# Weight matrices laid out partition by partition in DRAM, in a two-stage transformer kernel on eight cores

## The reference

```
mod = silu(c) @ wmod                       # six vectors per sequence: sa, ca, ga, sb, cb, gb
h = layernorm(x) * (1 + ca) + sa
x = x + ga * ttt(h)       # K, V, Q = h @ thetas; scan with W, b updated per token
h = layernorm(x) * (1 + cb) + sb
x = x + gb * ffn(h)
  ttt step:  g = 2/1024 * (W k + b - v);  W -= 0.01 * outer(g, k);  b -= 0.01 * g;  out = W q + b
  ffn:       routed = top-2 of 8 experts, y = (silu(h @ gate) * (h @ up)) @ down, weighted by the softmax scores
             shared = the same with matrices of inner width 2048
```

## Time and profile before

| | us |
|---|---|
| median of three runs | 1615.85 |
| the three runs | 1603.39, 1615.85, 1644.12 |
| the profiled execution | 1616.92 |
| its span, slowest core (core 3) | 1615.3 |
| cores 1, 5, 7 (second role) | 1612.0, 1609.5, 1596.2 |
| cores 0, 2, 4, 6 (first role) | 1535.8, 1546.6, 1536.4, 1550.9 |

### The profile page before, as it was taken

One profiled execution on the slowest core, in us unless ns is written; L12 is line 12 of the kernel. 1 busy time (PEld: TensorE's weight loads), 2 busy tenths in 40 slices (PEclk: granted clock), 3 DMA queues, 4 the chain that ended last, 5 costly groups with the idle time before them and its releaser, 6 DMA issues.

```text
span 1615.3 us, 22747 instructions; the slowest of 8 cores (1535.8 to 1615.3 us)
## 1 busy us (share of the span) xinstructions
PE 1417.2 (88%) x7825; PEld 703.9 (44%) x7825; DVE 738.8 (46%) x1278; ACT 493.8 (31%) x784; POOL 304.0 (19%) x209
## 2 busy tenths in 40 slices
PE   0587899798968998999997899999797999989897
PEld 0343444344444444444543444644343444434354
DVE  2426555647444456457447423432122222222576
ACT  1144444345444444444434321122121111101010
POOL 0058875803300001001011110000000000000131
PEclk9999999899989999999998999999899999999999
DMA  9954356616457522122172659397999999974763
GB/s 238 265 114 136 105 151 125 156 53 169 85 131 137 157 66 92 53 92 76 43 170 92 169 126 239 105 221 146 213 194 210 170 202 224 180 157 173 272 209 131
DMA packets 82373, 244.16 MB, mean 151 GB/s; under 512 B 7365, under 2 KB 7493, under 8 KB 77638
## 3 DMA queue, kind: packets, MB, share of 16 engines
q0 software_dynamic: 47440, 112.75, 35.2%
q1 hardware_dynamic: 26870, 92.05, 17.2%
q10 hardware_dynamic: 7936, 37.75, 9.5%
HBM read 262.46 MB, written 78.64 MB: 211 GB/s over the span
## 4 chain that ended last, share of the span: by engine, by line
PE 71%; DMA 13%; DVE 8%; issue 5%; POOL 1%; ACT 1%; another core or an unknown queue 1%; SPq 0%; DVEq 0%; POOLq 0%; ACTq 0%
PE prep L664 9%; PE u L928 7%; PE gate L897 5%; PE u L826 5%; PE up L897 5%; PE up L894 5%; PE gate L894 5%; PE prep L928 4%; PE up L729 3%; PE up L756 3%; DMA w1u<-uw 3%; PE gate L729 3%; DMA w1u<-suw 3%; PE gate L746 2%; DMA wmb<-wmod 2%
## 5 line engine op out<-in xcount | busy, mean ns | idle before, releaser
L1416 DVE TENSOR_TENSOR act<-up,sgb 128x512 bf16<-128x512 f32 (+1 forms) x128 | 84.0, 658 | 317.1 <-PE up L897 194.6
L1084 ACT ACTIVATE sgb<-gate 128x512 bf16<-128x512 f32 (+1 forms) x128 | 73.0, 570 | 466.1 <-PE gate L897 228.2
L1292 DVE TENSOR_TENSOR WT<-WT,u 128x512 f32<-128x512 f32 x240 | 153.4, 679 | 52.3 <-PE u L826 52.0
L826 PE MATMUL u<-Gsb,Ktk 128*128 128x512 bf16 x480 | 129.7, 394 | 41.9 <-DVE WT L1292 40.8
L664 PE MATMUL prep<-hft,s_thK 128*128 128x512 bf16 x512 | 124.3, 391 | 7.5 <-ACT hft L993 3.4
L1054 ACT CAST Wbf<-WT 128x1024 bf16<-128x1024 f32 x120 | 124.7, 1041 | 14.7 <-DVE WT L1292 14.6
L1603 POOL DMA_INDIRECT hx<-h2m,sl x28 | 29.1, 1038 | 447.4 <-DVE sl L1399 441.8
L826 PEld LDWEIGHTS u<-Gsb,Ktk 128*128 128x128 bf16 x480 | 44.0, 100 | 99.5 <-issue 63.9
L1545 POOL TENSOR_SCALAR x2b<-x2b,silc 128x1024 f32<-128x1024 f32 x28 | 80.1, 2862 | 23.6 <-DMA x2b<-wmod 22.5
L664 PEld LDWEIGHTS prep<-hft,s_thK 128*128 128x128 bf16 x512 | 50.5, 100 | 72.2 <-issue 18.9
L746 PE MATMUL gate<-Wbf,Kft 128*128 128x512 bf16 x256 | 80.8, 391 | 0.0
(11 more groups left out here) (250 smaller groups left out, 2318.2 us busy)
## 6 DMA issues: line engine op xcount, KB each, us to landing
hx<-zero ACTq DMA_DIRECT2D x4, 5120.0 KB, 30.6
x2b<-wmod POOLq DMA_DIRECT2D x32, 512.0 KB, 5.1
yx<-ring SPq DMA_DIRECT2D x32, 512.0 KB, 5.9
xb<-x SPq DMA_DIRECT2D x22, 512.0 KB
wmb<-wmod SPq DMA_DIRECT2D x8, 1024.0 KB, 12.1
x2b<-x SPq DMA_DIRECT2D x16, 512.0 KB, 4.6
hx<-zero ACTq DMA_DIRECT2D x4, 2048.0 KB, 11.4
pair<-gw POOLq DMA_DIRECT2D x4, 2048.0 KB, 29.2
```

Of the source, the lines that this page charges most:

```text
L826: m = t.matmul(U[jh][:, 0:512], Ktk[s % 2][:, cc * D + dt * P:cc * D + (dt + 1) * P], Gsb[:, cc * D + jh * 512:cc * D + (jh + 1) * 512], s ...
L1292: v.tensor_add(w, w, U[jh][:, 0:512]).then_inc(S["v_W"], 1)
L1416: v.tensor_mul(act[k % 2][:, fj * ACW:fj * ACW + COLS[k]], R[2 + n % 2][:, 0:COLS[k]], sgb[n % 2][:, 0:COLS[k]]).then_inc(v_act, 1)
```

## The change

The weight matrices are rearranged on the host: for each matrix `[1024, 1024]`, row `128 * dt + p` moves to row p, column `1024 * dt` of a matrix `[128, 8192]`. The shared matrices are first cut in halves. Each load then reads one contiguous run of 32 KB for each partition, and W0, loaded in two parts, runs of 16 KB. What arrives in SBUF, its place, the DMAs, their order and their waits stay as they are.

```diff
-    d_thK = nc.dram_tensor("thK", [D, D], F32, kind="ExternalInput")
+    d_thK = nc.dram_tensor("thK", [P, DT * D], F32, kind="ExternalInput")
...
-    d_gw = nc.dram_tensor("gw", [NE, D, D], F32, kind="ExternalInput")
-    d_sgw = nc.dram_tensor("sgw", [D, 2 * D], F32, kind="ExternalInput")
+    d_gw = nc.dram_tensor("gw", [NE, P, DT * D], F32, kind="ExternalInput")
+    d_sgw = nc.dram_tensor("sgw", [2, P, DT * D], F32, kind="ExternalInput")
...
                 for i in range(2):
                     g.dma_start(WT[:, 4 * i * D:4 * (i + 1) * D],
-                                ap(d_w0T, 4 * i * P * D, [[D, P], [P * D, 4], [1, D]])).then_inc(ld_w0, 16)
+                                ap(d_w0T, 4 * i * D, [[DT * D, P], [1, 4 * D]])).then_inc(ld_w0, 16)
...
                 def w_matrix(u, dst, which, done):
                     if u in (0, NE + 1):
-                        half = 0 if u == 0 else 1
-                        t, row, first = ((d_sgw, 2 * D, half * D), (d_suw, 2 * D, half * D),
-                                         (d_sdw, D, half * D * D))[which]
+                        t, i = (d_sgw, d_suw, d_sdw)[which], (0 if u == 0 else 1)
                     else:
-                        t, row, first = (d_gw, d_uw, d_dw)[which], D, (u - 1) * D * D
-                    g.dma_start(ap(dst, 0, [[DT * D, P], [D, DT], [1, D]]),
-                                ap(t, first, [[row, P], [P * row, DT], [1, D]])).then_inc(done, 16)
+                        t, i = (d_gw, d_uw, d_dw)[which], u - 1
+                    g.dma_start(ap(dst, 0, [[DT * D, P], [1, DT * D]]),
+                                ap(t, i * D * D, [[DT * D, P], [1, DT * D]])).then_inc(done, 16)
...
         def w_cast(g, dst, src, done):
-            g.dma_start(ap(dst, 0, [[DT * D, P], [D, DT], [1, D]]),
-                        ap(src, 0, [[D, P], [P * D, DT], [1, D]])).then_inc(done, 16)
+            g.dma_start(ap(dst, 0, [[DT * D, P], [1, DT * D]]),
+                        ap(src, 0, [[DT * D, P], [1, DT * D]])).then_inc(done, 16)
...
+    def by_partition(a):
+        a = np.asarray(a, dtype=np.float32)
+        t = a.reshape(a.shape[:-2] + (DT, P, D))
+        return np.ascontiguousarray(np.moveaxis(t, -3, -2)).reshape(a.shape[:-2] + (P, DT * D))
+    def halves(a, axis):
+        return np.stack(np.split(np.asarray(a, dtype=np.float32), 2, axis=axis))
```

More of the change, by code:

```diff
@@ L280, in build_program @@
     d_wmod = nc.dram_tensor("wmod", [D, 6 * D], F32, kind="ExternalInput")
-    d_thK = nc.dram_tensor("thK", [D, D], F32, kind="ExternalInput")
-    d_thV = nc.dram_tensor("thV", [D, D], F32, kind="ExternalInput")
-    d_thQ = nc.dram_tensor("thQ", [D, D], F32, kind="ExternalInput")
-    d_w0T = nc.dram_tensor("w0T", [D, D], F32, kind="ExternalInput")
+    d_thK = nc.dram_tensor("thK", [P, DT * D], F32, kind="ExternalInput")
+    d_thV = nc.dram_tensor("thV", [P, DT * D], F32, kind="ExternalInput")
+    d_thQ = nc.dram_tensor("thQ", [P, DT * D], F32, kind="ExternalInput")
+    d_w0T = nc.dram_tensor("w0T", [P, DT * D], F32, kind="ExternalInput")
     d_b0 = nc.dram_tensor("b0r", [1, D], F32, kind="ExternalInput")
     d_rw = nc.dram_tensor("rw", [D, NE], F32, kind="ExternalInput")
-    d_gw = nc.dram_tensor("gw", [NE, D, D], F32, kind="ExternalInput")
-    d_uw = nc.dram_tensor("uw", [NE, D, D], F32, kind="ExternalInput")
-    d_dw = nc.dram_tensor("dw", [NE, D, D], F32, kind="ExternalInput")
-    d_sgw = nc.dram_tensor("sgw", [D, 2 * D], F32, kind="ExternalInput")
-    d_suw = nc.dram_tensor("suw", [D, 2 * D], F32, kind="ExternalInput")
-    d_sdw = nc.dram_tensor("sdw", [2 * D, D], F32, kind="ExternalInput")
+    d_gw = nc.dram_tensor("gw", [NE, P, DT * D], F32, kind="ExternalInput")
+    d_uw = nc.dram_tensor("uw", [NE, P, DT * D], F32, kind="ExternalInput")
+    d_dw = nc.dram_tensor("dw", [NE, P, DT * D], F32, kind="ExternalInput")
+    d_sgw = nc.dram_tensor("sgw", [2, P, DT * D], F32, kind="ExternalInput")
+    d_suw = nc.dram_tensor("suw", [2, P, DT * D], F32, kind="ExternalInput")
+    d_sdw = nc.dram_tensor("sdw", [2, P, DT * D], F32, kind="ExternalInput")
     d_zero = nc.dram_tensor("zero", [P, D], BF16, kind="ExternalInput")
@@ L1897, in make_inputs @@
     f32 = lambda a: np.ascontiguousarray(np.asarray(a, dtype=np.float32))
+    def by_partition(a):
[4 more added lines that the diff above has]
+        return np.stack(np.split(np.asarray(a, dtype=np.float32), 2, axis=axis))
     base = {
[L1899 to L1902, removed]
+        "thK": by_partition(np.asarray(L0_attn_theta_K).T),
+        "thV": by_partition(np.asarray(L0_attn_theta_V).T),
+        "thQ": by_partition(np.asarray(L0_attn_theta_Q).T),
+        "w0T": by_partition(np.asarray(L0_attn_W0).T),
         "b0r": f32(np.asarray(L0_attn_b0).reshape(1, D)),
         "rw": f32(L0_ffn_router_w),
-        "gw": f32(L0_ffn_gate_w), "uw": f32(L0_ffn_up_w), "dw": f32(L0_ffn_down_w),
-        "sgw": f32(L0_ffn_shared_gate_w), "suw": f32(L0_ffn_shared_up_w),
-        "sdw": f32(L0_ffn_shared_down_w),
+        "gw": by_partition(L0_ffn_gate_w), "uw": by_partition(L0_ffn_up_w), "dw": by_partition(L0_ffn_down_w),
+        "sgw": by_partition(halves(L0_ffn_shared_gate_w, 1)), "suw": by_partition(halves(L0_ffn_shared_up_w, 1)),
+        "sdw": by_partition(halves(L0_ffn_shared_down_w, 0)),
         "wmod": f32(L0_wmod),
```

## The result

| | before | after |
|---|---|---|
| median, 20 runs each | 1614.49 us | 1627.60 us |
| ratio of the changed kernel to the kernel before | | 1.0075, 95% interval 1.0051 to 1.0100 |
| span of core 3, the slowest, in the profiled execution | 1615.3 us | 1625.0 us |

Within 2%, but clearly on the other side of no change than was forecast. The ratio is that of undisturbed executions; in others one die or both run at a lower granted clock and end some per cent later.

A forecast was written before the change was run, and what follows sets the result against it. The prediction took the second role's cores, with TensorE waiting for late expert weights, to bound the kernel. It summed -12.6 - 2.3 + 2 - 3 = -15.9, from 1616.9 to 1601 us, range 1578 to 1628 (8 in 10).

The forecast's parts named there:

- What bounds the kernel: Second role's cores end last; in the expert stage TensorE waits 18.4 us and 4.8 us for late w1u loads.
- (a) Cost per packet: Weight loads on POOL's queue: memory, not packets, sets the pace, so fewer packets save 0.
- (b) Share of turns: Late weight bursts beside SP and ACT: weights hold 86% of turns, waits shrink 12.6 us, slow matmuls behind them 2.3.
- (c) What waits longer, ring: x2 rows read back to the ring: a row tile stands behind weight turns, +2 us (0 to +8).
- (c) token rows: Experts' token-row loads behind weight turns: 42 us, then the rest runs free, within 46.3 us of cover; it fits.
- the prediction's own signs of being wrong: Lone burst's bytes per us move over 5%, TensorE waits at hxb's transposes, or VectorE's ring wait grows over 8 us.
- (d) The start: VectorE's modulation sums at the start: thK lands sooner, second wmod tile about 5 us sooner; -3 us, bounds -5 and +3.5.
- nothing changes: Rival for the whole kernel: runs cut again into some 4 KB packets, or memory's pace hides all; 1616 us, chance 0.28.
- slower memory order: Rival in weight bursts: reads from places 32 KB apart cost a sixth of the pace; +40, 1657 us, chance 0.09.
- Full relief: Rival in late bursts: long sequential reads win back the other 5 us, all waits go; -35.2, 1582 us, chance 0.17.
- Starved token rows: Rival in the experts: unpausing weight turns make token loads 57 us, +10 us in each of seven; 1672 us, chance 0.05.
- VectorE's wait for ring grows by more than 8 us: A sign that would show the prediction wrong, at VectorE's wait for x2 rows read back, 5.6 us once before.

The follow-up runs named there:

- e6: Changed kernel, but only thK, thV, thQ and W0 keep long runs; expert and shared matrices in separated 4 KB rows; ratio to the kernel before 0.9975.
- e3: Changed kernel's layout with a 256 B gap behind each 4 KB row, so no read is longer; ratio to the kernel before 0.9997.
- e4: Changed kernel with units 1 and 2 (first two experts) in separated 4 KB rows, other matrices in 32 KB runs; 1599.4 us, 0.9899 of the kernel before.
- e9: Changed kernel with e1's three waits on POOL's queue and each partition's token rows made one piece; ratio to the kernel before 0.9921.
- e1: Changed kernel with three more waits on POOL's queue, issuing weights of units 1 and 2 later, apart from x2 tiles; 1607.6 us, 0.9970 of the kernel before.

## Why the prediction was wrong, point by point

- **What bounds the kernel**: right. The late bursts were TensorE's only DMA waits of size in the expert part, and they went: 23.2 to 3.7 us.
- **(a) Cost per packet, taken as 0**: right, as far as it shows: 4.5 to 5.7 MB in 30 us of a burst before, 4.6 to 5.7 after.
- **(b) Share of turns, -12.6 and -2.3**: the mechanism was right, the turns are one for one, and beside SP and ACT the queue moved 4.92 MB in 36 us against 4.75 in 30 nearly alone, 86%, the forecast share. It measured -19.5 us of waits and, in the experts' stretch, -13.2 with the wait of 3.2 us for hxb in it. The forecast took 4.2 us from each late burst; measured, all but 3.7 us of the 23.2 went, so the weights' share of the turns was worth about half as much again. Why it is more than the turns account for I did not separate; that a burst no longer begins late behind another late one is argued only. That a wait as short as 0.6 us spares the slow matmuls held: behind the wait of 0.3 us for `w0u` eight took 1.89 us, the usual time in this timeline. Behind 3.41 us they took 3.54.
- **(c) What waits longer, ring, +2 (0 to +8)**: here it failed. The wait for ring grew by 28.0 us and the stage by 28.6. The sum priced one tile, eight packets per engine, against weights that it took for passing by. At the first place SP has five tiles queued, 40 packets per engine, beside 24 long turns, and one of its tiles lands only at 950.27 + 44.57 = 994.8 us. The sum counted 24 turns for the token rows and only eight here; with 24 x 1.77 = 42 us it would have had this wait. At the second, the finished tile in a place of the ring must be written out before the next is read into it, both through SP's queue beside the next burst: 28.9 us from issue to landing, a wait of 20.3. The row that it rested on, 5.6 us, was read as a bound on the effect, though it only showed how little was to spare.
- **(c) token rows, no cost**: nearly. 24 x 1.77 = 42 us was the forecast for a landing behind a whole burst; 42.6 was measured once, with 3.2 us of wait. But the cover of 46.3 us was that of a step with a wait of 9.7 us and its slow matmuls in it. In a plain step it is 34.2: issue at 1194.53, first transpose at 1228.74 in the kernel before. At the place of the new wait it was 39.6, since the wait for `w1u` fell into it, and the load took 42.6. That TensorE waits there was one of the prediction's own signs of being wrong.
- **(d) The start, -3**: wrong in sign, small in size. thK did land sooner (20.0 us for 29.5), but by the code SP's queue has five loads of eight packets per engine (the first x rows and four of constants) ahead of the first wmod tile, and they too take turns with thK: the x rows let VectorE start some 3.5 us later, the tile came at 27.7 and not at 21.5. The wait before the second tile fell to 2.8, as forecast, only because the first came late. No run separated this. The sums end at 61.0 us in place of 58.4, 2.6 later, and the difference is lost in the scatter of the scan (947.2 against 949.3). e6 shows no loss.
- **The rivals**: *nothing changes* failed at the packet count; *slower memory order* failed at e3 and at the pace of the bursts. *Full relief* nearly had its end, 3.7 us of weight waits left, but not by its reason, since the bursts' pace did not change. *Starved token rows* had the right mechanism at the wrong place: it was the x2 tiles that starved, in the stage before, and no rival put it there. The forecast's own doubt of "VectorE's wait for ring grows by more than 8 us" is what came true.

## What to carry to other kernels

When a transfer gets longer packets, write down every other queue that is active beside it, and price each of its waiting packets with one long turn; count all the packets that are queued at that moment, not those of one transfer. A wait of a few us on the small side in the profile of before is a warning and not a bound. Here 4 KB reads already moved at the pace of 32 KB ones, so a longer run was only a way to shift shares between queues: worth about 1% where it is kept from the x2 tiles (e4, e9), and at 32 KB a loss where it is not.

## What the runs showed of the hardware

- POOL's queue does not cut a contiguous casting run: 32 KB read and 16 KB written are one packet, and a software queue of 47440 packets becomes one of 17104.
- What a wait of TensorE costs behind it is not fixed by its length. Eight matmuls, 1.89 us in a plain stretch of the timeline, took 3.54 behind a wait of 3.4 us in the changed kernel and 3.04 behind one of 2.2 in e9 (core 3), but 1.89 behind one of 3.7 in e1 (core 1). In the stretch behind the first the granted clock was 0.78.
- POOL's own time per issue fell from 0.88 to 0.54 us with 128 packets in place of 1024 (0.87 in the earlier trace rows, and this row of the changed kernel):

```profile
1354.88 0.53 POOL L1577 DMA_DIRECT2D w1d<-dw  x1 [41.63 <-PE u L928]
```

- The Trainium skill (DMA: Bandwidth & Descriptors, SWDGE vs HWDGE vs iDMA) wants packets of this queue at 4096 B preferably. The measured ones are four times that after the cast; the measurement decides.
